# First four tiles mixed by fourths in another load order, and half of the weight sums moved from GpSimd to VectorE

## The reference

```python
def ternary_project(w, threshold=0.05):
    scale = jnp.mean(jnp.abs(w), axis=0, keepdims=True)
    return jnp.where(jnp.abs(w) < threshold, 0.0, jnp.sign(w)) * scale

# x: (32, 64, 1024) float32, itok: (32,) of 0..15
W = L0_cond_weights[itok]                       # (32, 64, 64)
y = jnp.einsum('bct,bcd->bdt', x, W)            # mixes the 64 channels of each batch
x = x + y @ ternary_project(L0_ffn_w) + L0_ffn_b
W = L1_cond_weights[itok]
y = jnp.einsum('bct,bcd->bdt', x, W)
w = (NF4_LEVELS[q_weight].reshape(-1, 64) * q_scale[:, None]).reshape(1024, 1024)
x = x + jnp.einsum('bsi,oi->bso', y, w) + bias + 4.0 * (y @ lora_A.T) @ lora_B.T
```

## Time and profile before

| | |
|---|---|
| median of 3 runs | 344.71 us |
| the profiled execution | 344.56 us |
| its span | 342.5 us |
| PE busy | 332.4 us (97%) |
| PEld busy | 271.4 us (79%) |
| DVE busy | 236.0 us (69%) |
| ACT busy | 164.5 us (48%) |
| POOL busy | 245.0 us (72%) |
| HBM | 25.40 MB read, 14.68 MB written |

### The profile page before, as it was taken

The page is one execution under the profiler, slowest core; times in us unless marked ns, Lnnn a source line. Parts: engine busy times, 40 slices in busy tenths (PEclk is TensorE's granted clock), DMA queues, the critical chain, the costliest instruction groups (busy, mean ns, idle before and its releaser), DMA issues.

```text
span 342.5 us, 8187 instructions
## 1 busy us (share of the span) xinstructions
PE 332.4 (97%) x3142; PEld 271.4 (79%) x3142; DVE 236.0 (69%) x356; ACT 164.5 (48%) x300; POOL 245.0 (72%) x160
## 2 busy tenths in 40 slices
PE   7999999989999999999799999999999999999996
PEld 6868778778888778887678888888888888888884
DVE  7787567899999999999999736346263462624623
ACT  1799357877897787788171403214032140411400
POOL 0298999998896896986578966766467664677642
PEclk9999999999999999999999999999999999999999
DMA  6894511644354245300100151412513124150302
GB/s 229 291 341 132 201 33 33 271 168 159 118 167 162 93 157 177 141 10 13 55 2 3 65 189 63 150 44 74 181 65 131 63 84 169 67 169 23 124 31 92
DMA packets 25800, 40.60 MB, mean 119 GB/s; under 512 B 7810, under 2 KB 16002, under 8 KB 25762
## 3 DMA queue, kind: packets, MB, share of 16 engines
q1 hardware_dynamic: 25090, 39.48, 33.3%
q10 hardware_dynamic: 672, 0.61, 0.5%
HBM read 25.40 MB, written 14.68 MB: 117 GB/s over the span
## 4 chain that ended last, share of the span: by engine, by line
PE 51%; DVE 20%; POOL 12%; issue 8%; ACT 4%; DMA 1%; SPq 1%; DVEq 0%; POOLq 0%; ACTq 0%
PE acc L1268 45%; POOL col_scale L631 4%; DVE hl L914 3%; DVE ys L941 3%; POOL x_first L604 3%; PE spare L1154 2%; PE xT L1154 2%; POOL x_first L611 2%; DVE side_n L953 2%; ACT spare L762 2%; DVE W L988 2%; DMA w_in<-in_L_ffn_w 1%; POOL side_p L638 1%; DVE side_p L953 1%; DVE side_n L956 1%
## 5 line engine op out<-in xcount | busy, mean ns | idle before, releaser
L1268 PE MATMUL acc<-W,hh 128*128 128x512 f32 x256 | 81.4, 389 | 0.0
L1228 PE MATMUL acc<-T,hh 128*128 128x512 f32 x192 | 76.5, 398 | 0.0
L1228 PE MATMUL acc<-T,hl 128*128 128x512 f32 x192 | 75.0, 391 | 0.0
L604 POOL TENSOR_TENSOR X<-X,bias 128x1024 f32<-128x1024 f32 x28 | 68.1, 2432 | 0.0
L762 ACT ACTIVATE spare<-q_raw 128x512 f32<-128x512 int32 x96 | 56.1, 599 | 20.2 <-DVE side_n L953 5.0
L1040 DVE TENSOR_TENSOR X<-X,acc 128x512 f32<-128x512 f32 x48 | 32.9, 685 | 36.7 <-PE acc L1268 28.9
L1268 PEld LDWEIGHTS acc<-W,hh 128*128 128x128 f32 x256 | 48.0, 188 | 10.0
L663 POOL TENSOR_TENSOR X<-X,ys 128x512 f32<-128x512 f32 x24 | 30.5, 1299 | 34.1 <-DVE ys L1029 34.1
L1268 PE MATMUL acc<-W,hl 128*128 128x512 f32 x128 | 49.8, 389 | 0.0
L797 ACT ACTIVATE hh<-xT 128x512 fp32r<-128x512 f32 x16 | 8.7, 595 | 77.6 <-PE xT L1154 77.6
L1228 PEld LDWEIGHTS acc<-T,hh 128*128 128x128 f32 x192 | 36.0, 188 | 8.0
(11 more groups left out here) (98 smaller groups left out, 606.5 us busy)
## 6 DMA issues: line engine op xcount, KB each, us to landing
out<-X SPq DMA_DIRECT2D x22, 512.0 KB, 3.1
X<-in_x SPq DMA_DIRECT2D x12, 512.0 KB, 3.4
X<-out SPq DMA_DIRECT2D x12, 512.0 KB, 3.8
q_raw<-in_L_ffn_q_weight SPq DMA_DIRECT2D x16, 256.0 KB, 2.9
w_in<-in_L_ffn_w SPq DMA_DIRECT2D x14, 256.0 KB, 6.8
x_first<-in_x SPq DMA_DIRECT2D x4, 512.0 KB, 5.1
out<-x_first SPq DMA_DIRECT2D x4, 512.0 KB, 4.6
out<-X SPq DMA_DIRECT2D x4, 256.0 KB, 2.0
```

The source lines that it names most:

```text
L604: pool.tensor_tensor(x_of(g), x_of(g), bias[:, :], ALU.add).then_inc(s_xb, 1)
L1228: mm = pe.matmul(acc[:, bank_of(q), :], a[:, k, :], T0[:, n, k, :], start=(k == 0 and j == 0), stop=(k == KB - 1 and j == 1))
L1268: mm = pe.matmul(acc[:, bank, :], a[:, k, :], w1(part, c, k), start=(k == 0 and j == 0), stop=(k == HB - 1 and j == len(terms) - 1))
```

## The change

- Tiles 0 to 3 are mixed with `mixed_batches` too; `mixed` goes away. High and low parts of all tiles have the same layout now, and a tile is ready as a whole, not by halves. Tile 1 goes to two banks of `acc`, the others to `xT`.
- `first(g, n, start, stop)` takes any range of blocks, and the order on PE changes: blocks 0 and 1 of tile 0 come directly after the mix of tile 1, then the tiles take turns by two blocks. Seven more unused products: `WARM` is 7, one stands behind `turn_b` and four behind the mix of tile 0.
- SyncE loads x of tile 1 later, and no longer the matrices of tiles 2 and 3; POOL issues these four loads after tile 0 has arrived, under their own semaphores. ACT's share of them goes away as well. The weights and x of tiles 2 and 3 move up.
- ACT copies the second half of the turned `lora_b` instead of DVE.
- `sums` on POOL covers the first half of the columns only. DVE adds the absolutes of the second half, one block after each ternary block (`add_absolute`), in the PSUM tile `flat(1)`, the last one into `col_scale`. In POOL's list `add_bias(3)` moves up.
- The plan of lines and maxima: weights 5 for the first eight halves, 10 for 18, 6 for three. `turned_in` becomes `max(NH * F + d, ready_in(d) + 2)`. `colscale(1)` stands before the lines of tile index 2 instead of 1.

```diff
-    WARM = 5
+    WARM = 7
...
+    SHARES = [5] * (NH * F) + [10] * 18 + [6] * 3
     def share(total, m):
-        m = min(m, NH * NT - 3)
-        whole = 3 * NH * F + 10 * (NH * (NT - F) - 3)
-        return total * (3 * min(m, NH * F) + 10 * max(0, m - NH * F)) // whole
+        return total * sum(SHARES[:m]) // sum(SHARES)
...
-        return max(NH * F, ready_in(d) + 2)
+        return max(NH * F + d, ready_in(d) + 2)
...
         def batch(g, s):
+            if g == 1:
+                return acc[:, 2 + s, :].rearrange("p (k c) -> p k c", k=KB)
...
+        def matrices(eng, g):
+            if g in (2, 3):
+                eng.wait_ge(s_mix_early[g], 32)
+            else:
+                eng.wait_ge(s_mix[g % NM], 32 * (g // NM + (g % NM < 2)))
...
             load_x(0)
-            load_x(1)
             sp.wait_ge(s_tok, 16)
             sp.wait_ge(s_fill, 1)
             load_condition(sp, 0, 0)
+            load_x(1)
             load_condition(sp, 1, 0)
+            load_weights(sp, 1, 0)
             load_x(2)
-            load_condition(sp, 2, 0)
-            load_weights(sp, 1, 0)
             load_weights(sp, 3, 0)
-            load_condition(sp, 3, 0)
             load_weights(sp, 4, 0)
+            load_weights(sp, 5, 0)
             load_x(3)
-            load_condition(sp, 3, 1)
-            load_weights(sp, 5, 0)
...
-            sums(0, 1, KB)
-            sums(1, 1, KB)
+            pool.wait_ge(s_tok, 16)
+            pool.wait_ge(s_fill, 1)
+            pool.wait_ge(s_x0[0], 16)
+            for g in (2, 3):
+                for s in range(2):
+                    load_condition(pool, g, s)
+            sums()
             add_bias(0)
             result_half(0)
             add_bias(1)
             result_half(1)
+            add_bias(2)
             pool.wait_ge(s_scales, 16)
-            add_bias(2)
+            add_bias(3)
             result_half(2)
             for m in range(NH * F - 3):
                 weights_of(m)
-            add_bias(3)
...
-            load_condition(act, 2, 1)
+            act.wait_ge(s_bT, 2)
+            act.activation(lora_columns(1), lora_turned(1), ACT.Copy).then_inc(s_loraB, 1)
             high_x(0, 0)
             high_x(0, 1)
             signs(0, 2)
             absolute(0, 2)
+            high_x(1, 0)
+            high_x(1, 1)
             signs(0, 3)
             absolute(0, 3)
-            high_x(1, 0)
-            high_x(1, 1)
...
             for g in range(SB):
-                if g == 1:
+                if g == 2:
                     colscale(1)
...
+            def add_absolute(k):
+                if k == 0:
+                    return
+                dve.wait_ge(s_abs, KB + k + 1)
+                out = col_scale[:, BANK:T] if k == KB - 1 else flat(1)
+                if k == 1:
+                    dve.wait_ge(s_hl, NH * F)
+                    ins = dve.tensor_tensor(out, w_raw(0, 1), w_raw(1, 1), ALU.add)
+                else:
+                    dve.wait_ge(s_added, k - 1)
+                    ins = dve.tensor_tensor(out, flat(1), w_raw(k, 1), ALU.add)
+                ins.then_inc(s_added, 1)
...
             low_x(0, 1)
             ternary(0, 1)
+            low_x(1, 0)
+            low_x(1, 1)
             ternary(0, 2)
             ternary(0, 3)
-            low_x(1, 0)
-            low_x(1, 1)
+            low_x(2, 0)
+            low_x(2, 1)
             ternary(0, 4)
-            low_x(2, 0)
             ternary(0, 5)
-            low_x(2, 1)
...
             for k in range(4):
                 ternary(1, k)
+                add_absolute(k)
             leave_y(0)
             leave_y(1)
             for k in range(4, KB):
                 ternary(1, k)
+                add_absolute(k)
...
+            idle(WARM)
             turn_b()
-            mixed(0)
-            mixed(1)
-            mixed(2)
-            first(0, 0, 0)
-            first(1, 0, 0)
-            mixed(3)
-            first(0, 0, 1)
-            first(1, 0, 1)
+            idle(1)
+            mixed_batches(0)
+            idle(4)
+            mixed_batches(1)
+            first(0, 0, 0, 2)
+            mixed_batches(2)
+            first(1, 0, 0, 2)
+            first(0, 0, 2, 4)
+            first(1, 0, 2, 4)
+            first(2, 0, 0, 4)
+            first(0, 0, 4, 6)
+            mixed_batches(3)
+            first(1, 0, 4, 6)
+            first(2, 0, 4, 6)
+            first(0, 0, 6, KB)
+            first(1, 0, 6, KB)
+            first(2, 0, 6, KB)
+            first(3, 0, 0, HB)
             column_sums(0)
-            first(2, 0, 0)
-            first(2, 0, 1)
-            first(3, 0, 0)
-            first(3, 0, 1)
-            first(0, 1, 0)
-            first(0, 1, 1)
-            first(1, 1, 0)
+            first(3, 0, HB, KB)
+            first(0, 1, 0, HB)
+            first(1, 1, 0, HB)
+            first(0, 1, HB, KB)
+            first(1, 1, HB, KB)
             column_sums(1)
-            first(1, 1, 1)
-            first(2, 1, 0)
-            first(2, 1, 1)
+            first(2, 1, 0, KB)
             mixed_batches(F)
-            first(3, 1, 0)
-            first(3, 1, 1)
+            first(3, 1, 0, KB)
```

More of the change, by code:

```diff
@@ L1131, in _ @@
         def _(pe):
-            def mixed(g):
-                pe.wait_ge(s_mix[g % NM], 32 * (g // NM + 1))
-                arrived(pe, g)
-                if g == 2 or g == 3:
-                    pe.wait_ge(s_hl, NH * (g - 1))
-                for k in range(KB):
-                    mm = pe.matmul(turned(g, k // HB)[:, k % HB, :], x_of(g)[:, k * P:(k + 1) * P],
-                                   mix[:, g % NM, :], start=True, stop=True)
-                    if k % HB == HB - 1:
-                        mm.then_inc(s_xT, 1)
             def quarters(g, turn):
```

90 lines of the change are left out of this document (43 added, 47 removed).

## The result

The kernel after took 347.37 us (median of 4 runs, 346.97 to 351.3) against 344.69 us before (344.63 to 344.8, 4 runs), a ratio of 1.0111 [1.0082, 1.0139]. The later sets of runs, on other chips, put the kernel before at 343.98 to 344.49 us and the kernel after at 347.33, 2.9 us above the kernel before beside it. The forecast was 343.3 us with a range up to 345.8: the change makes the kernel slower by 2.7 us, and the time lies outside the range. The profiled execution of after took 347.01 us, its span is 344.9 us, 2.4 more than the span before.

The account below looks back on a forecast made before the run. PE was taken as the bound (busy 97% of the span), with VectorE the second bound in `main`. The sum was 344.56 + 2.0 (later `main`) - 4.0 + 0.7 (stalls) = 343.3 us, range 340.6 to 345.8.

Parts of the forecast that it names:

- + 2.0 (later `main`): Ahead of `main`: VectorE's added work before `low_x(4)` makes `main` start 2.0 us later, at 53.0 and not 50.99 us.
- First product at 11.4 us: Start of the kernel, on PE: the first real product starts near 11.4 instead of 13.77 us.
- POOL's matrices at zero: Start: POOL issuing the matrices of tiles 2 and 3 costs zero, with up to 3 us in the range.
- Rival (d): Start: VectorE keeps POOL from writing what its DMAs need, so tile 2's matrices are late; 3 us, 346.3 us; chance 0.05.
- First half done at 29.7 us: First four tiles: the 64 products of the first half end at about 29.7 us, against 32.8 before, a 3.1 us lead.
- Additions at 4.2 us, hidden in part: Second half of tiles 0 to 3: seven additions cost VectorE 4.2 us, partly hidden in its 7.4 us of waiting.
- Six maxima at 4.4 us, of which part is hidden: Ahead of `low_x(4)`: 14 maxima and not 8 cost VectorE 4.4 us, partly hidden in its own waiting.
- `colscale(1)` at 43.2 with a wait of 1.7 us: ACT's queue, behind 11 lines instead of 3: `colscale(1)` comes at 43.2 us, PE arrives at 41.5 and stands 1.7 us.
- `main` at 53.0: Walk through VectorE's queue: `low_x(4)` ends at 51.8 us and `main` starts at 53.0 and not 50.99 us.
- Stalls of `main` 4.0 to 0.7: In `main`: VectorE's smaller lag cuts PE's idle time from 4.0 to 0.7 us, bounds 0 and 3.
- Products unchanged: From 170.94 us to the end: PE is busy 168.37 of 171.56 us, and nothing in this change is there.
- Rival (c): VectorE's queue up to `mixed_batches(5)`: `low_x(4)` becomes the gate, `main` starts at 55.4, 346.0 us, slower; chance 0.12.

Follow-up runs that it names:

- `loraA` copy: After, with the low part of `loraA` computed from a copy ACT puts into PSUM, in two steps with one input there: 346.91 us, ratio 1.0077.
- after again: The kernel after, unchanged, run once more beside the kernel before: 347.33 us, ratio 1.0083.

## Why the prediction was right or wrong: where the 2.7 to 2.9 us come from

The kernels make a ladder in which each step is one part. The medians come from different chips, so the steps are taken between the distances to the kernel before beside each. They carry an uncertainty of half to one us, and the spans are of one execution each:

| kernel | median, us | against before beside it | step | span of the trace, us | step |
|---|---|---|---|---|---|
| before | 343.98 to 344.69 | 0 | | 342.5 | |
| + additions on VectorE | 342.36 | -2.1 | -2.1 | 340.3 | -2.2 |
| + new order of tiles 0 to 3, fourths, unused products | 342.01 | -2.5 | -0.4 | 340.9 | +0.6 |
| + new shares | 346.08 | +2.1 | +4.6 | 343.1 | +2.2 |
| + matrices issued by POOL (= after) | 347.33 to 347.37 | +2.7 to +2.9 | +0.6 to +0.8 | 344.9 | +1.8 |

The steps depend on each other: with the old shares POOL's matrices cost 3.5 us (from -2.5 to +1.0), and then the new shares 1.7 to 1.9. In either order the shares and the matrices take 5.2 to 5.4 us, and the rest of the change gives 2.5. How the 5.3 us divide between the two is less sure than their sum. The new order, the fourths and the unused products were only once taken apart (without the unused products, nothing to be told); their row stands for all three.

**The shares.** They take maxima out of `main`, and its lost time (119.8 against 115.1 us) vanishes. But the six extra maxima stand before `low_x(4)`, where VectorE has nothing left to hide them in, since the additions have already taken its idle time. PE waits 5.1 us longer there (5.4 and 0.3 in the fence above), `main` starts 4.85 later, and 3.4 us (matrices on SyncE) of it come back in `main`; with the matrices on POOL it was 4.2, of which 2.6 are idle time and the rest a fall of the clock. A lighter end costs on top: from first to last product the seven traces with share 6 in the last three portions take 168.9 to 169.2 us, six of the seven with 10 take 167.9 to 168.2 (the seventh, the second execution of before, 169.4 with a gap of 1.0 us in it). In after the trace shows where, on VectorE, then on POOL:

```profile
166.44 6.60 DVE L1014 TENSOR_TENSOR W<-W_sums,W 128x512 fp32r<-128x512 f32 x5
172.96 0.68 DVE L967 TENSOR_TENSOR ys<-acc,col_scale 128x512 f32<-128x512 f32 x1
```

```profile
165.49 2.38 POOL L632 TENSOR_TENSOR X<-X,ys 128x1024 f32<-128x1024 f32 x1 [3.12 <-DMA bias<-in_L_ffn_bias]
167.84 2.84 POOL L619 TENSOR_TENSOR X<-X,bias 128x1024 f32<-128x1024 f32 x1
```

The five low sums (L1014, both inputs in SBUF) take 6.60 us. POOL began its pair 0.95 us ahead of them; with the old shares (matrices on SyncE) it begins 2.7 us ahead (161.44, VectorE 164.18), less of it lies beside them, and they take 4.90. `leave_y` stands behind them, and PE waits 0.7 us for its bank (the row at L1282 above).

**The start.** The new order gives a first product at 10.1 to 10.3 us with the matrices on SyncE, about 2 us earlier than the old one with as early a clock (12.13 and 12.71), and yet the head is no shorter: 23.4 to 24.9 us in five traces against 22.7 to 23.6 in three of the old order. The second half's signs stand on ACT behind the split of tile 3, and the fourths of tile 3 now stand behind 14 block products and not 8: at 19.4 to 20.9 us (22.28 in after), in the old order at 16.8 to 18.1. The lead at the start is thus no lead at the place that counts; only a shorter queue (25.7 us with the old shares) makes up for it. With POOL's loads the head is 24.2 to 28.2 us in six traces, longest where the clock fell to half near 15 us.

## Why the prediction was right or wrong, point by point

The step that failed is the term "+ 2.0 (later `main`)": it measured +6.2 us, while the stalls gave back 4.7 and not 3.3. The gate was the one named, `low_x(4)` in VectorE's queue. What was wrong is when VectorE would get there: it came to the second half 2.2 us later than walked (POOL's matrices at nothing, and PE's waits for blocks and splits), and its queue from there was 2.0 us longer (the `loraA` step, left at its old length).

- **First product at 11.4 us**: 9.98. Right in kind, 1.4 us too careful. The fill products had no visible part in it (10.60 without them, 9.98 to 10.68 with them).
- **POOL's matrices at zero**: my dear end had them landed near 12.5 us, and PE's mix of tile 2 waited for them until 12.55. It was no zero, for a reason other than the dear issues: each takes 1.14 to 1.2 us from start to start, as the 1.2 us of the earlier trace rows, but the first stands at 6.37 us and not 4.6, behind the load of tile 0. The wait itself is 0.45 us; behind it come the gap and the half clock. With the matrices on SyncE the head is 1.7 us shorter and the time 0.6 to 0.8 us (new shares) to 3.5 us (old shares). Rival (d) had the place and a price of 3 us, at 0.05; its mechanism, VectorE keeping POOL from writing, was not seen: VectorE's operations take 0.69 us beside POOL's issues as elsewhere, and POOL issues at SyncE's pace.
- **First half done at 29.7 us**: 32.7 (4 products after the column sums at 29.85). My walk had a lead of 3.1 us; 0.5 (before: 33.2) was left. Of the missing 3.0, 1.7 is gone with POOL's matrices (31.0 there), the rest is PE waiting for ternary blocks and splits that I had put at nothing.
- **Additions at 4.2 us, hidden in part**: the size was right (0.60 each, the first 1.35 long: 0.7 more, the foreseen surcharge). They are hidden wholly: before, plus the additions alone, is 2.1 us faster. The bound of 5.7 us for seven additions of the dear kind was summed wrongly (seven times 0.8 more is 9.8), which changed nothing in the forecast. The Trainium skill ("SBUF — State Buffer", "Who interferes with whom") gave the right rule for these, and the trace agrees: the additions with one input in PSUM at 33.51 and 34.71 us take 0.69 us beside POOL. I did not carry it one line further: L1083, `loraA`, has both inputs in SBUF as well, and once the additions are off POOL, POOL is at the bias beside it. 1.25 us became 3.20. That is the largest single miss in the queue, and taking one input from PSUM brings it back to 1.30.
- **Six maxima at 4.4 us, of which part is hidden**: 4.4 us measured too (0.73 each), and 0.8 us of longer waiting for `col_scale` on top, and nothing hidden. I had let 8.6 us of new work draw on 7.4 us of waiting, of which 2.5 were to stay. The additions and the longer `loraA` step used that up alone. That budget, 8.6 less 4.9, already asked for a queue 3.7 us longer than before; the walk let it grow by 1.5 only (see `main`), and it grew by 3.6. Ahead of `main` stand 15 maxima, not 16.
- **`colscale(1)` at 43.2 with a wait of 1.7 us**: at 47.06 with 2.2. Mechanism and size right, but all 4 us later. It was never the gate on its own, since `hl` follows.
- **`main` at 53.0**: 57.23. The walk has ACT at the second half's first sign at 22.8 us. Before, that sign stood at 22.33 us and not one sign ahead of 23.50, and the first ternary block 1.3 us behind it (23.63), so the walk's block stands at 24.1 and its queue is 28.9 us (27.4 before). Measured are 25.00, 26.30 and 30.9: 2.2 of the 4.2 us come from the head, 2.0 from the queue, as much as the `loraA` step has grown (1.95).
- **Stalls of `main` 4.0 to 0.7**: to 0.2, and the stretch is 4.66 us shorter and not 3.3. Right in mechanism, 1.4 us too little.
- **Products unchanged**: +0.8. I had said that nothing of the change was in that stretch; what is left of `main` in VectorE's queue was.
- **The sum** had its sign from two terms, +2.0 and -3.3. With the measured ones it is +6.2, -4.7 and +0.8. Rival (c) named the right gate, "VectorE's queue between `leave_y(2)` and `mixed_batches(5)`", the right rule (each us there moves everything) and a start of `main` of 55.4; it got 0.12 because I priced it by hand-overs and not by the terms that did it. My own note that `main`'s start was the term I trusted least should have widened the range to its end: with `main` at 55 and stalls at 0.7 the sum already gives 345.3.

## What to carry to other kernels

Work moved to an idle stretch of an engine uses that stretch once: when two parts of a change are both to be hidden in the same waits, subtract the first before pricing the second. When work leaves an engine early, list every operation that now runs beside its later work, and look for those on the other engine with both inputs in SBUF. And judge a faster start at the first point where the engines meet again, not at its first product.

## What the runs showed that I had not expected

- **DMAs issued by POOL.** They take 0.52 to 0.69 us each to issue (first and last of four below), SyncE's 0.47 to 0.58, and 5.4 us in the median to land, against 4.2 for SyncE's four in the same stretch of the kernel with the matrices on SyncE. The queues moved 347 GB/s in the one and 307 in the other, so the issuing engine is not the only difference. POOL's timeline, and the issues from 5 to 16 us of after and of that kernel (columns: what, queue, number, KB each, median us to landing):

```profile
6.37 0.69 POOL L485 DMA_DIRECT2D mix<-in_L_cond_weights  x1 [4.77 <-issue]
...
9.85 0.52 POOL L485 DMA_DIRECT2D mix<-in_L_cond_weights  x1 [0.63 <-issue]
```

```profile
mix<-in_L_cond_weights POOLq DMA_DIRECT2D x4, 16.0 KB, 5.4
```

```profile
mix<-in_L_cond_weights SPq DMA_DIRECT2D x4, 16.0 KB, 4.2
```

- **A gap of "issue" on PE in mid-mix.** It came after the 57th of 64 records in four of the six traces with POOL's loads: both of after (1.15 and 1.87 us), the one with the additions on POOL (1.15) and the one with the `loraA` copy (0.66). The old shares and the kernel without the unused products have POOL's loads and no gap; the kernels with the matrices on SyncE have none there. A fetch of 16 KB on the instruction queue, 0.9 to 1.2 us long, began at 12.4 to 13.5 us in the four and at 10.5 to 11.5 with the matrices on SyncE; with the old shares (POOL's loads) it was over at 13.2 us and the mix began at 13.97. That the gap is PE waiting for this fetch fits, but no run takes the fetch away, so it stays open.
- **The clock falls for a few us in some executions.** In after it was half from 14.84 to 18.25 and from 48.97 to 52.38 us, 0.06 and 1.07 us behind the end of a wait of PE (1.15 and 2.19 us), and the 16 records of `first` at 48.99 took 5.52 us and not 3.92. The same gap of 1.15 us passed without a fall in the kernel with the additions on POOL. A wait of 3.2 us ahead of the fourths of tile 5 was followed by a fall within 1.1 us in three traces (`loraA` copy, no unused products, after again) and by none in the kernel with the matrices on SyncE. So a wait does not always bring it, and one of the costs of a stall here is a fall that may follow, about 1.6 us for each. The 19 runs of before beside one set of kernels lie within 2.2 us of each other, the first four of after within 4.3, and four of the five later ones within 3.0.
- **Two SBUF inputs cost both sides, by the overlap.** VectorE's 64x1024 subtraction went from 1.25 to 3.20 us and POOL's two operations beside it from 4.8 (two of 2.4) to 5.72. The first addition took 0.69 us where POOL was idle (all five kernels with the matrices on SyncE, and before with the additions), 1.35 in after, where POOL's 2.41 us of bias lay over its first 0.8 us, and 2.58 in the kernel without the unused products, where it lay over the first 2.0.
